# Mamba stage: transposes of the scanned state as ordinary fp32 matmuls with the identity

## The reference

```python
dA = jnp.exp(delta[..., None] * -jnp.exp(a_log))
mi = ALPHA * delta[..., None] * Bm[:, :, None, :] * xb[..., None]

def scan_fn(carry, inp):
    h, v = carry
    dA_t, mi_t, C_t = inp
    v = BETA * v + mi_t
    h = dA_t * h + v
    y_t = jnp.einsum('ben,bn->be', h, C_t)
    return ((h, v), y_t)
...
y = ys.transpose(1, 0, 2) + dp * xb
y = y * jax.nn.silu(z)
return jnp.einsum('ble,de->bld', y, ow)
```

## Time and profile before

| | us |
|---|---|
| median of three runs | 5296.98 |
| lowest and highest run | 5295.73 and 5300.83 |
| the profiled execution | 5273.95 |
| its span | 5272.2 |
| TensorE matmul busy | 3926.8 |
| VectorE busy | 3440.9 |
| ScalarE busy | 2424.4 |

### The profile page before, as it was taken

The page is one execution under the profiler, slowest core; times in us unless marked ns, Lnnn a source line. Parts: engine busy times, 40 slices in busy tenths (PEclk is TensorE's granted clock), DMA queues, the critical chain, the costliest instruction groups (busy, mean ns, idle before and its releaser), DMA issues. The chain is left out here.

```text
span 5272.2 us, 119189 instructions
## 1 busy us (share of the span) xinstructions
PE 3926.8 (74%) x41100; PEld 3133.2 (59%) x41101; DVE 3440.9 (65%) x6074; ACT 2424.4 (46%) x4814; POOL 1818.8 (34%) x1826
## 2 busy tenths in 40 slices
PE   6888799288888888888578778888788721788880
PEld 3555466276676676767456667677676621566660
DVE  3444422588888888888578888888888763333334
ACT  1111122266666566665465666656666520223320
POOL 1001000245445454454344544544545424000006
PEclk9888789587787787777677877777787755999995
DMA  1000000100000000000000000000000052100003
GB/s 42 0 0 0 18 0 0 46 2 2 2 2 2 2 2 2 2 2 2 15 2 2 2 2 2 2 2 2 2 2 2 1 215 76 41 30 30 30 27 96
DMA packets 50238, 93.91 MB, mean 18 GB/s; under 512 B 8946, under 2 KB 35442, under 8 KB 47028
## 3 DMA queue, kind: packets, MB, share of 16 engines
q1 hardware_dynamic: 40116, 60.89, 3.3%
q0 software_dynamic: 9600, 26.23, 1.5%
HBM read 51.42 MB, written 35.65 MB: 17 GB/s over the span
## 5 line engine op out<-in xcount | busy, mean ns | idle before, releaser
L922 DVE TENSOR_TENSOR_SCAN m_h<-m_dA,m_hlast,m_bank 128x256 f32<-128x256 f32 x2048 | 1358.9, 725 | 52.5 <-PE m_bank L1192 31.4
L1175 PE MATMUL m_bank<-ident,m_h 128*128 128x128 f32 x4096 | 739.2, 328 | 396.4 <-ACT m_prod L1048 191.1
L1192 PE MATMUL m_bank<-m_Mlo,m_Uhi 80*128 80x64 bf16 x8192 | 973.1, 210 | 61.0 <-issue 25.0
L1192 PE MATMUL m_bank<-m_Mhi,m_Ulo 80*128 80x64 bf16 x8192 | 969.0, 210 | 5.7 <-issue 5.7
L1192 PE MATMUL m_bank<-m_Mhi,m_Uhi 80*128 80x64 bf16 x8192 | 968.9, 210 | 0.0
L1192 PEld LDWEIGHTS m_bank<-m_Mlo,m_Uhi 80*128 80x128 bf16 x8192 | 844.8, 109 | 106.0 <-issue 45.0
L1038 ACT ACTIVATE m_dA<-m_delta,m_rate 128x256 f32<-128x256 f32 x2064 | 878.6, 501 | 32.8 <-issue 25.2
L1192 PEld LDWEIGHTS m_bank<-m_Mhi,m_Ulo 80*128 80x128 bf16 x8192 | 844.9, 110 | 45.4 <-issue 25.8
L1175 PEld LDWEIGHTS m_bank<-ident,m_h 128*128 128x128 f32 x4096 | 549.1, 167 | 497.4 <-issue 192.7
L1192 PEld LDWEIGHTS m_bank<-m_Mhi,m_Uhi 80*128 80x128 bf16 x8192 | 842.3, 109 | 0.0
L786 POOL TENSOR_TENSOR m_y<-m_y,m_prod 128x512 f32<-128x512 f32 x480 | 642.3, 1338 | 419.0 <-ACT m_prod L1048 419.0
(11 more groups left out here) (274 smaller groups left out, 7353.7 us busy)
## 6 DMA issues: line engine op xcount, KB each, us to landing
g_stage<-in_e_w SPq DMA_DIRECT2D x16, 1024.0 KB, 6.8
slots_x<-x_res SPq DMA_DIRECT2D x36, 256.0 KB, 7.4
x_x_in<-slots_x SPq DMA_DIRECT2D x72, 128.0 KB, 2.0
slots_y<-x_y POOLq DMA_DIRECT2D x72, 128.0 KB, 2.0
x_res<-in_x SPq DMA_DIRECT2D x1, 4096.0 KB, 13.9
parked<-x_res SPq DMA_DIRECT2D x1, 4096.0 KB, 13.5
so_residual<-parked SPq DMA_DIRECT2D x1, 4096.0 KB, 14.8
out_x<-x_res SPq DMA_DIRECT2D x1, 4096.0 KB, 13.6
```

Source lines behind the costliest of these rows:

```text
L922: nc.vector.tensor_tensor_scan(h[:, n % 3, m, :], dA[:, n % 3, m, :], VB[(n % 2) * 2 + m // 2][:, (m % 2) * CM:(m % 2 + 1) * CM], hlast[:, ...
L1175: last = nc.tensor.transpose(HB[tt][:, m * P:(m + 1) * P], h[:, n % 3, m, tt * P:(tt + 1) * P], net.ident[:])
L1192: last = nc.tensor.matmul(bank[:, at:at + SUB], u_part[:, par, jj, m * P:(m + 1) * P], m_part[:, par, jj, n, :], start=(i == 0), stop=(i = ...
```

## The change

In `turn`, each of the eight blocks of a state is issued as a matmul with the state's block as weights and the identity as the streamed operand, with start and stop set, in place of a transpose with the same operands. Banks, buffers, order and semaphores stay.

```diff
                         for m in range(KI):
-                            last = nc.tensor.transpose(HB[tt][:, m * P:(m + 1) * P],
-                                                       h[:, n % 3, m, tt * P:(tt + 1) * P], net.ident[:])
+                            last = nc.tensor.matmul(HB[tt][:, m * P:(m + 1) * P], h[:, n % 3, m, tt * P:(tt + 1) * P],
+                                                    net.ident[:], start=True, stop=True)
                         last.then_inc(s["ht_psum"], 1)
```

## The result

The changed kernel takes 5439.72 us (median of four runs, 5405.61 to 5443.61), the kernel before 5296.35 us: a ratio of 1.026, with a 95% interval of 1.0215 to 1.0305, so some 138 to 143 us more. It lies in rival 1's range, 5385 to 5475, and so in the wide one that was to hold four times in five, 5385 to 5800.

The account below looks back on a forecast made before the run. VectorE was taken to set the pace in plain slots, with waits for TensorE around the next chunk's preparation. Path terms summed to 8.5 us a chunk, times 32 chunks +273 us: 5570, own range 5475 to 5655, wide range 5385 to 5800.

Parts of the forecast that it names:

- rival 1: TensorE: ordinary matmuls count more as activity than transposes and bring its clock back sooner; +122 us, 5420 (5385 to 5475), chance 0.17.
- Rivals 3 and 4: Transposed blocks: either four steps each, near 6680 us, chance 0.02; or no change, 5297 us, chance 0.05.
- The price of a turn: Eight blocks of one state on TensorE cost 0.9 us more at 2.4 GHz, 1.7 at 1.2 GHz.
- Rival 2: TensorE becomes the bound and every turn is paid, some perhaps half; 5655 to 5870 us, chance 0.20.
- The five places: Turns of a chunk said to lie on the path, where VectorE or the output projection waits for TensorE.
- states 2, 3 and 4: Around the output and input projections, before the convolution: +0.88 us a chunk for state 2, +1.8 for 3 and 4.
- States 8 and 9: Before the two small projections, after which VectorE waits 0.60 us: +1.65 us a chunk.
- States 14 and 15: Cold turns around the carry matmuls, for which VectorE waits: +2.4 us a chunk, between 1.8 warm and 3.4 cold.
- States 10 and 11: Turns in a cold stretch: +1.5 us a chunk, the middle between 0 and 3.1 depending on the clock.
- the other nine states: States 0, 1, 5, 6, 7, 12, 13 and remainders of 2 and 8, covered by VectorE's scans: +0.3 us a chunk.
- Rival 5: Faster: the clock effect also covers the output projection, sixteen steps ending some 2.2 us earlier; 5255 us, chance 0.06.
- The signs I had named: Profile after: longer waits at projection, convolution, clamp, carries; chunks 101 to 107 us; VectorE busy unchanged; clock over 0.88 refutes.

Follow-up runs that it names:

- f3: Kernel before, with ordinary matmuls only for the seven hidden states (0, 1, 5, 6, 7, 12, 13), transposes for the rest: 5218 us, ratio 0.9847.
- h4: Kernel before, with ordinary matmuls for the seven hidden states and states 8 and 9: 5246 us, ratio 0.9923.
- h3: Kernel before, with ordinary matmuls for the seven hidden states and states 2, 3 and 4: 5273 us, ratio 0.9974.
- f2: Kernel before, with ordinary matmuls only for the nine path states (2, 3, 4, 8, 9, 10, 11, 14, 15): 5439 us, ratio 1.0266.
- f1: Kernel before, with every block of all 16 states transposed twice, none as ordinary matmul: 5402 us, ratio 1.0192.
- h2: Kernel before, with ordinary matmuls for the seven hidden states and states 14 and 15: 5245 us, ratio 0.9920.
- i3: Kernel before, with only states 0 and 1, ahead of the output projection, transposed twice: 5235 us, ratio 0.9886.
- f4: Kernel before, with four unused fp32 matmuls in TensorE's idle time ahead of state 2's second half, before the output projection: 5286 us, ratio 0.9985.

## Why the prediction was right or wrong, point by point

**Right.** An ordinary fp32 matmul is two records, not one and not four: 8192 records at 275 ns. Rivals 3 and 4 are out. The price of a turn, 0.9 us, was 0.96. Slower by more than 0.2% was right. VectorE's plain slots kept their pace where I had named no cost: scan at 1795.63 and next scan at 1798.85 in the changed kernel, 3.22 us, and 3.21 in the median after states 3, 8 and 14. After state 5 the median rose from 3.22 to 3.70 and after state 10 from 3.22 to 5.11, both places of the sum. Rival 2, which needs every turn to be paid, is out: the transposes' waits have not vanished, they went from 396 to 324 us.

**Luck in the range.** 5385 to 5800 holds the time, but by rival 1's part of it. The forecast's own case missed, at about half of its +273, and by its own sign: it was to be wrong with a mean clock in a chunk over 0.88, and that is 0.90 to 0.91.

**The five places.** Forecast against measured over f3: states 2, 3 and 4: 0.88 + 1.8 = 2.7 us a chunk, 86 us, measured 67. States 8 and 9: 1.65, 53, measured 40. States 14 and 15: 2.4, 77, measured 39, even less than two warm turns (1.8, 58). States 10 and 11: 1.5, 48, measured 71, or 2.2 us a chunk; that is too low by a third, with an uncertainty of 0.6 us a chunk. Together 263 forecast, 217 measured. The traces, read as in the table of stretches, show that a place can cost what was said and the clock give some of it back elsewhere. Over f3, h4 is 1.84 us a chunk longer from state 10 to 12 (said: 1.65), and 1.3 shorter at the projection and at the carries. h3 is 1.92 longer at the convolution (said: 1.8), and 0.11 shorter at the projection, where I had put 0.88 for state 2.

**The step that failed** is what a clock that is up for longer gives back: it stood in the sum at nothing. I treated the clock as something that changes the price of states 10, 11, 14 and 15, and left its effect on all other TensorE work out of the likeliest case. It sat in rival 1, with a chance of 0.17. It shows most plainly in the line on the other nine states, "covered by VectorE's scans", with +0.3 us a chunk: seven of them, doubled alone, save 0.0153 x 5290 = 81 us, 2.5 us a chunk. -81 + 217 = 136 us: this closes the account with the measured +138 (ratio) to within the intervals. It is not the only way to share it out: the nine alone cost 141 us (f2), where the sum had 263, and the seven then add nothing. In either order the gain of the clock is had once, and is missing from the sum. Not all of the 81 is the clock: VectorE's shorter copies are 0.77 us a chunk of it, 25 us.

**Rival 1** had the time (5420) and one place of the gain, the cold end of the chunk (1.28 us a chunk in f3; the projection, which it left out, gave 0.97). It had the wrong reason: ordinary matmuls were to count more than transposes. f1 shows that what matters is that TensorE is given work for longer, in either mode; by f2 and h2, the place of the work counts too. The Trainium skill, "TensorE: Matmul & The Clock Gate", Part 4, says that the full clock does not engage for transposes; here the clock rises as far with 8192 transposes (0.852) as with 8192 ordinary records (0.856). The row that I set against that rule had said so, and I should have drawn the other half from it: if transposes count, more of them count too.

**Rival 5** named the projection at 2.4 GHz as the point that decides. f3 and i3 show that this does come about, and is worth some 30 to 37 us of VectorE's waits; for all sixteen states the price was larger. f4, aimed at that wait alone, took 29 us off it and gained 8 us (0.15%): a wait that goes is not yet time that goes.

**The signs I had named.** Waits before the convolution and the clamp: up by 1.2 and 1.5 us a chunk, as said. The wait behind the projection: said to rise by 0.9 us, fell by 0.2. The carries: said to rise, fell. Chunks of 101 to 107 us: 99.4 and 101.8, and 100.5 in the mean of all. The scans' waits for velocity (31 to 93 us) I had not put into the sum at all: the turn ahead of a velocity is longer, and after state 8's turn and the projection of line 1099 the scan of state 11 waits:

```profile
1807.80 2.66 DVE L922 TENSOR_TENSOR_SCAN m_h<-m_dA,m_hlast,m_bank 128x256 f32<-128x256 f32 x4 [1.81 <-PE m_bank L1192]
```

VectorE's busy time was to stay, and fell by 20 us. The mean clock in a chunk was to stay under 0.88, or else rivals 1 and 5 would hold; it is 0.90 to 0.91.

## What to carry to other kernels

Before pricing a change to TensorE, write down which of its stretches run at 1.2 GHz and which engine waits behind each: added work in a covered place right before such a stretch can pay for itself, and here seven turns of useless transposes made the kernel 1.9% faster. Then look at the whole period, since in f4 the clock that was gained in one stretch was lost in another. Price a doubled instruction at each place apart: two turns more, 1.9 us of work, cost 2.2 us a chunk for states 10 and 11, 1.3 for 8 and 9, and less than nothing for 12 and 13 (doubled transposes). When a rival's mechanism and a row speak against each other, ask what the row says about the effect itself, not just about the reason given for it.

## What the runs showed of the hardware that was not expected

- TensorE's clock did not depend on the mode of the work in `turn`: 0.781 with 4096 transposes, 0.852 with 8192, 0.856 with 8192 ordinary records. It did depend on the place of it: with 6400 records it is 0.808 in f2 and 0.849 in h2.
- Two of sixteen turns doubled (states 12 and 13, or 0 and 1) were enough for 1.4 and 1.1%.
- The same small bf16 copy on VectorE takes 1.05 us with a sum on POOL beside it and 0.28 us without, in all fourteen traces.
